# The first cumulative sum of gates: from a TensorE product to a VectorE scan, in the gated stage of a four-layer kernel

## The reference

```python
gk1 = log_sigmoid(x @ Wg1a @ Wg1b + bg1) / 16      # decays of the dense branch, 8 heads x 64
gk2 = log_sigmoid(x @ Wg2a @ Wg2b + bg2) / 16      # of the four routed branches
def chunk_gla(q, k, v, gk, C=64):                  # chunks of 64 tokens
    g = cumsum(gk, axis=1)                         # inside a chunk
    g_last = g[:, -1]
    qg, kg = q * exp(g), k * exp(-g)
    A = tril(qg @ kg.T)
    ...
    return S * exp(g_last) + kv                    # state to the next chunk
o = chunk_gla(q1, k1, v, gk1) + sum_e chunk_gla(q2*w_e, k2*w_e, v, gk2*m_e)
```

## Time and profile before

| | |
|---|---|
| median of three runs | 1802.73 us |
| the profiled execution | 1806.19 us, span 1804.9 us |
| granted TensorE clock, mean over the span | 0.951 |
| TensorE matmul busy | 1556.2 us (86%) |
| VectorE busy | 1275.3 us (71%) |
| ScalarE busy | 1098.3 us (61%) |
| GpSimd busy | 697.8 us (39%) |

### The profile page before, as it was taken

The page is one execution under the profiler, slowest core; times in us unless marked ns, Lnnn a source line. Parts: engine busy times, 40 slices in busy tenths (PEclk is TensorE's granted clock), DMA queues, the critical chain, the costliest instruction groups (busy, mean ns, idle before and its releaser), DMA issues. The chain is left out here.

```text
span 1804.9 us, 45554 instructions
## 1 busy us (share of the span) xinstructions
PE 1556.2 (86%) x19648; PEld 998.5 (55%) x19648; DVE 1275.3 (71%) x2003; ACT 1098.3 (61%) x1641; POOL 697.8 (39%) x499
## 2 busy tenths in 40 slices
PE   3587897899999999999977778888788888899999
PEld 2354566787778778877863232433333343466565
DVE  4656644777777677768767868778777886655665
ACT  3255576777767777786752567677667767533331
POOL 4122300554255344534450556365465545411100
PEclk8789898999999999999997889999999999999999
DMA  7864200000000000000024274246237222223332
GB/s 176 196 165 113 47 5 12 2 2 2 2 2 2 2 1 2 2 1 2 32 88 99 52 212 98 63 133 142 56 107 167 66 64 72 67 71 94 95 96 76
DMA packets 54821, 121.17 MB, mean 67 GB/s; under 512 B 6124, under 2 KB 14468, under 8 KB 53020
## 3 DMA queue, kind: packets, MB, share of 16 engines
q1 hardware_dynamic: 51708, 112.74, 23.7%
q10 hardware_dynamic: 2912, 5.51, 1.8%
HBM read 85.70 MB, written 31.74 MB: 65 GB/s over the span
## 5 line engine op out<-in xcount | busy, mean ns | idle before, releaser
L1445 DVE TENSOR_REDUCE arena<-ring 128x2 f32<-128x1024 f32 (+2 forms) x320 | 342.1, 1110 | 87.9 <-PE ring L1302 62.1
L1545 ACT ACTIVATE arena<-ring 128x1024 f32<-128x1024 f32 (+1 forms) x320 | 291.3, 937 | 135.4 <-PE ring L1331 92.0
L1352 PE MATMUL accs<-arena 128*9 128x512 f32 (+3 forms) x1536 | 174.3, 528 | 3.8 <-ACT arena L1545 3.8
L2509 POOL TENSOR_TENSOR arena<-arena 128x1280 f32<-128x1280 f32 x28 | 65.3, 2332 | 287.0 <-PE accs L2270 231.7
L1295 PE MATMUL ring<-arena 48*128 48x512 bf16 (+3 forms) x768 | 128.8, 347 | 41.8 <-DVE arena L1445 21.1
L1324 PE MATMUL ring<-arena 51*128 51x512 bf16 (+3 forms) x768 | 125.0, 343 | 45.8 <-DVE arena L1445 25.1
L2501 POOL TENSOR_TENSOR arena<-arena 128x512 f32<-128x512 f32 x112 | 141.3, 1294 | 3.0 <-DVE arena L2311 3.0
L287 POOL TENSOR_SCALAR xn<-x,moments,rstd 128x128 f32<-128x128 f32 x80 | 65.0, 825 | 192.3 <-DVE rstd L258 178.3
L2782 ACT ACTIVATE arena<-ring 128x512 f32<-128x512 f32 x80 | 47.7, 596 | 134.8 <-PE ring L2651 132.7
L2494 POOL TENSOR_TENSOR arena<-arena 128x1024 f32<-128x1024 f32 x32 | 86.3, 2698 | 108.1 <-DVE arena L2368 108.1
L1718 POOL TENSOR_TENSOR arena<-arena 128x1024 f32<-128x1024 f32 x28 | 65.9, 2354 | 128.6 <-ACT arena L1558 104.5
(11 more groups left out here) (342 smaller groups left out, 4165.9 us busy)
## 6 DMA issues: line engine op xcount, KB each, us to landing
arena<-whole_k SPq DMA_DIRECT2D x32, 512.0 KB, 4.6
arena<-whole_q SPq DMA_DIRECT2D x32, 512.0 KB, 6.2
arena<-moe_scratch SPq DMA_DIRECT2D x128, 128.0 KB, 2.9
arena<-c_scratch_q SPq DMA_DIRECT2D x14, 384.0 KB, 9.3
arena<-c_scratch_k SPq DMA_DIRECT2D x14, 384.0 KB, 12.2
a_scratch_k<-arena SPq DMA_DIRECT2D x8, 512.0 KB, 4.2
c_scratch_k<-arena SPq DMA_DIRECT2D x8, 512.0 KB, 4.5
arena<-a_scratch_q SPq DMA_DIRECT2D x9, 384.0 KB, 7.2
```

What stands on the lines that cost most here:

```text
L1352: mm = nc.tensor.matmul(acc[ci % 2][32 * h:32 * h + HD + 1, a - c * BANK:BANK], c_values[b % 2][:, j, r * HEADS // 2 + 2 * g + i, :], weig ...
L1445: nc.vector.tensor_reduce(dst, src, AX.X, ALU.max, negate=True).then_inc(c_max_taken.up(item), 1)
L1545: nc.scalar.activation(view(c_probs[wi % 4]), view(ps), ACT.Exp).then_inc(c_weights_made.up(item), 1)
```

## The change

Tile by tile, the first gate is now projected with features on partitions: `z` keeps one matmul of 512 columns for the second gate (L1925) and has four of 128 columns with the operands swapped for the first (L1928). `gk` is unchanged in shape. A new item `run`, VectorE's alone, stands behind `pair` and makes the cumulative sums in place with a scan over tokens: a reduction of each pair's first 64 tokens, its subtraction from the first token (four elements a partition), and a 512-element scan with a mask that restarts it at each pair (L2328, L2331, L2334). `sum, t, 0` has no TensorE part and no ring buffer any more; ScalarE's part reads the scan's result from SBUF, at the same place of the list, and its decays are two instructions. `gk` waits for ScalarE's last read of the tile before. GpSimd sets the mask once.

```diff
@@ z, on TensorE
-                for i in range(2):
-                    rows = slice(64 * (1 - h) + 32 * i, 64 * (1 - h) + 32 * i + 32)
-                    mm = nc.tensor.matmul(ps[:, i * BANK:(i + 1) * BANK], low_of(b, h)[rows, 1, in_half(t)],
-                                          w("b_second", (1 + h) * BANK, (2 + h) * BANK)[rows, :], start=True, stop=True)
+                rows = [slice(64 * (1 - h) + 32 * i, 64 * (1 - h) + 32 * i + 32) for i in range(2)]
+                low = low_of(b, h)[:, 1, in_half(t)]
+                up_gates = w("b_second", (1 + h) * BANK, (2 + h) * BANK)
+                nc.tensor.matmul(ps[:, BANK:2 * BANK], low[rows[1], :], up_gates[rows[1], :], start=True, stop=True)
+                for p in range(PAIRS):
+                    cols = slice(p * P, (p + 1) * P)
+                    mm = nc.tensor.matmul(ps[:, cols], up_gates[rows[0], cols], low[rows[0], :], start=True, stop=True)
...
@@ gk, on VectorE
                     dv.wait_ge(sum_mm, (t - 1, 1))
+                    dv.wait_ge(sum_exp, (t - 1, 0, "decay"))
...
@@ the order
-                round_ = [("pair", i), ("half", n), ("sc", i, 0), ("sc", i, 1), ("k2x", n), ("mx", n), ("mask", i),
+                round_ = [("pair", i), ("run", n), ("half", n), ("sc", i, 0), ("sc", i, 1), ("k2x", n), ("mx", n), ("mask", i),
                           ("sum", n, 0), ("kt", i), ("soft", n), ("fin", i - 1), ("sum", n, 1), ("qk1", n), ("vk", n),
                           ("z", n + 1), ("routed", n), ("kv", i, 0), ("kv", i, 1), ("av", i), ("in", i, 0), ("in", i, 1),
                           ("mid", n), ("gk", n + 1)]
-            on_ring = ("turn", "logits", "rows_hot", "rows_w", "low", "gate", "z", "mx", "vk", "sum", "qk1", "pair", "kt",
+            on_ring = ("turn", "logits", "rows_hot", "rows_w", "low", "gate", "z", "mx", "vk", "qk1", "pair", "kt",
                        "kv", "fin")
...
@@ run, on VectorE
+                    elif kind == "run":
+                        dv.wait_ge(z_step, (t, "gk"))
+                        by_pair = gk[:, 0, :].rearrange("p (a c) -> p a c", a=PAIRS)
+                        nc.vector.tensor_reduce(gk_head[:, :], by_pair[:, :, 0:P // 2], AX.X, ALU.add).then_inc(
+                            z_step.up((t, "head")), 1)
+                        dv.wait_ge(z_step, (t, "head"))
+                        nc.vector.tensor_tensor(by_pair[:, :, 0], by_pair[:, :, 0], gk_head[:, :], ALU.subtract).then_inc(
+                            z_step.up((t, "begin")), 1)
+                        dv.wait_ge(z_step, (t, "begin"))
+                        nc.vector.tensor_tensor_scan(gk[:, 0, :], pair_keep[:, :], gk[:, 0, :], 0.0, ALU.mult, ALU.add).then_inc(
+                            z_step.up((t, "running")), 1)
...
@@ sum 0, on ScalarE
+                    elif kind == "sum" and item[2] == 0:
+                        running = gk[:, 0, :]
+                        ac.wait_ge(z_step, (t, "running"))
+                        if t:
+                            ac.wait_ge(qk_decayed, (t - 1, "k1"))
+                        nc.scalar.activation(up[0][:, :], running, ACT.Exp, scale=1 / NORMALIZER).then_inc(
+                            sum_exp.up((t, 0, "up")), 1)
+                        nc.scalar.activation(dn[0][:, :], running, ACT.Exp, scale=-1 / NORMALIZER).then_inc(
+                            sum_exp.up((t, 0, "down")), 1)
...
+                        nc.scalar.activation(decay[t % 3][:, :, 0, 0], pair_cols(running)[:, :, P - 1], ACT.Exp,
+                                             scale=1 / NORMALIZER).then_inc(sum_exp.up((t, 0, "end")), 1)
+                        nc.scalar.activation(decay[t % 3][:, :, 1, 0], gk_head[:, :], ACT.Exp, scale=1 / NORMALIZER).then_inc(
+                            sum_exp.up((t, 0, "decay")), 1)
```

More of the change, by code:

```diff
@@ L1842, in build @@
         xnT_1 = carve([P, T])
+        pair_keep, gk_head = carve([P, BANK]), carve([P, PAIRS])
         assert used[0] <= SHARED
@@ L1969, in gla_first_dve @@
                     dv.wait_ge(sum_mm, (t - 1, 1))
+                    dv.wait_ge(sum_exp, (t - 1, 0, "decay"))
+                else:
+                    dv.wait_ge(gla_cleared, "pair first")
                 z = ps[:, :].rearrange("p (i c) -> p i c", i=2)
@@ L2067, in beside @@
                 return {k: more.get(k, []) + follow.get(k, []) for k in (*more, *follow)}
-            order = [("z", 0), ("pair", -1), ("gk", 0), ("half", 0), ("k2x", 0), ("mx", 0), ("sum", 0, 0), ("soft", 0), ("sum", 0, 1),
+            order = [("z", 0), ("pair", -1), ("gk", 0), ("run", 0), ("half", 0), ("k2x", 0), ("mx", 0), ("sum", 0, 0), ("soft", 0), ("sum", 0, 1),
                      ("qk1", 0), ("vk", 0), ("z", 1), ("routed", 0), ("gk", 1)]
@@ L2091, in gla @@
             for item in order:
-                if item[0] in on_ring or item[0] == "sc" and item[2] == 0 or (
+                if item[0] in on_ring or item[0] == "sc" and item[2] == 0 or item[0] == "sum" and item[2] == 1 or (
                         item[0] == "next" and item[1] in ("turn", "q", "k")):
@@ L2196, in pe_program @@
                         mm.then_inc(pair_mm.up(t), 1)
[L2197 to L2200, removed]
+                    elif kind == "sum" and item[2] == 1:
                         pe.wait_ge(z_step, (t, "gk"))
-                        if i:
-                            pe.wait_ge(mix_made, (t, "sum"))
-                            pe.wait_ge(mix_half, t)
+                        pe.wait_ge(mix_made, (t, "sum"))
+                        pe.wait_ge(mix_half, t)
                         for p in range(PAIRS):
-                            mm = nc.tensor.matmul(ps[:, p * 256:p * 256 + cols], gk[:, i, p * P:(p + 1) * P], rhs,
+                            mm = nc.tensor.matmul(ps[:, p * 256:p * 256 + P + 2 * ROUTES], gk[:, 1, p * P:(p + 1) * P], mixed[:, :],
                                                   start=True, stop=True)
-                        mm.then_inc(sum_mm.up((t, i)), 1)
+                        mm.then_inc(sum_mm.up((t, 1)), 1)
                     elif kind == "qk1":
@@ new lines, in act_program @@
+                        nc.scalar.activation(decay[t % 3][:, :, 1, 0], gk_head[:, :], ACT.Exp, scale=1 / NORMALIZER).then_inc(
+                            sum_exp.up((t, 0, "decay")), 1)
+                    elif kind == "sum":
+                        v4 = pair_cols(ps[:, :])
+                        ac.wait_ge(sum_mm, (t, 1))
+                        if t:
+                            ac.wait_ge(qk_decayed, (t - 1, "q2"))
+                        nc.scalar.activation(pair_cols(up[1][:, :]), v4[:, :, 0:P], ACT.Exp).then_inc(
+                            sum_exp.up((t, 1, "up")), 1)
+                        nc.scalar.activation(pair_cols(dn[1][:, :]), v4[:, :, 0:P], ACT.Exp, scale=-1.0).then_inc(
+                            sum_exp.up((t, 1, "down")), 1)
+                        if t >= 3 and last_factor(t - 2):
+                            ac.wait_ge(state_step, (last_factor(t - 2), "factor"))
+                        nc.scalar.activation(decay[t % 3][:, :, :, 1:1 + ROUTES],
+                                             v4[:, :, P:P + 2 * ROUTES].rearrange("p a (k d) -> p a k d", k=2),
+                                             ACT.Exp).then_inc(sum_exp.up((t, 1, "decay")), 1)
@@ L2489, in pool_program @@
             def pool_program():
+                nc.gpsimd.memset(pair_keep[:, :], 1.0).then_inc(gla_cleared.up("pair keep"), 1)
+                gp.wait_ge(gla_cleared, "pair keep")
+                nc.gpsimd.memset(pair_cols(pair_keep[:, :])[:, :, 0:1], 0.0).then_inc(gla_cleared.up("pair first"), 1)
                 for item in order:
```

17 lines of the change are left out of this document (2 added, 15 removed).

## The result

The changed kernel takes 1886.74 us (median of six runs, 1885.82 to 1898.08), the kernel before 1803.13 us in the same comparison (six runs): ratio 1.0479, 95% interval 1.0441 to 1.0517. It is slower by 84 us; 61 were forecast (1864 us). The range given eight chances in ten went to 1893; the forecast's own range ended at 1885, and 1886.74 lies just outside it and inside that of rival 3, the clock (1878 to 1910). The forecast had the sign, the place and some three quarters of the size.

What follows compares the result with a forecast made beforehand. VectorE's leg from second queries to first keys, then TensorE's back, bound it; terms of 15.1 us a batch gave 60.5 us on 1806.19, 1866.7, less 3.5 for the median: 1864 us; own range 1845 to 1885, eight in ten 1826 to 1893.

Steps and rivals of the forecast that it cites:

- rival 3: In the gated stage TensorE's clock falls in the new idle stretch: 1878 to 1910 us in all; 20% chance.
- The lock: VectorE instructions with two SBUF operands stand still until GpSimd's current one ends: `run` 2.9 us instead of 1.8.
- The sum, tile by tile: Growth of each tile's round in the gated stage, added up: 15.1 us a batch, 60.5 us for four batches.
- TensorE's new wait for the first mask: Before `fin`, which now reuses the first scores' buffer: start at x + 6.1 instead of x + 4.13, some 3 us idle.
- TensorE just about keeps up with VectorE: After the wait TensorE reaches `kv` at x + 13.3 to 13.5, with VectorE's first keys ending at x + 13.5.
- what it saved comes out as idle time: TensorE's four removed 130-column sums, 1.02 us a round, were to become idle time on TensorE.
- Tile 5's term: Tile 5's round, taken to have some slack: between 0 and 1.9 us longer, put at 1.25.
- the rival's milder form: A third of the rounds lose 1 to 1.7 us from `fin` to `kv` by the slower clock: 11 to 18 us more.
- Two signs that the prediction named as "wrong": Granted clock well under 1.00 in the gated stage; VectorE waiting in front of the first keys. No size given.
- The upper bound of 0.43: Extra time of `z` on TensorE if half of the second band's work is serialised: 0.43 us; 0.1 was taken.
- TensorE as the bound from the start: TensorE bounds the kernel and each round gets 0.6 to 0.9 us shorter: 1774 to 1784 us; 5% chance.
- No lock on the new instructions: `run` on VectorE isn't held up by GpSimd and takes 1.85 us: 28 us more, 1831 us; 14% chance.

Runs made afterwards that it cites:

- the filled kernel: The changed kernel with the eight transposes of `kt` done three times, 1.74 us more TensorE work a round before the first mask: 1869.52 us, ratio 1.0381.

## Why the prediction was right, and where not

- **What bounds the kernel.** Right: VectorE's leg to the first keys, against 94% on TensorE. Moving `run` out of it gave back 71 us, and shortening the leg of the kernel before gained 10 us without removing any work.
- **The lock.** Right, and the walk held to 0.2 us: scan's end 4.91 for 4.95, keys 13.32 for 13.5. That the leg grows by less than the 2.9 us of `run`, because L2408 no longer waits, was right too: 1.8 us (13.32 less 11.55) for the forecast 1.9.
- **The sum, tile by tile.** By how much a round is longer than before, in us; "full clock" is from rounds of the changed kernel without a fall of the clock, or, for tiles 1, 5 and 7, from such rounds of the filled one:

| tile of the batch | forecast | full clock | changed kernel |
|---|---|---|---|
| 0 | 1.9 | 1.8 | 1.8 (0.2 in the first batch) |
| 1 | 3.3 | 3.0 | 2.8 to 4.8 |
| 2 | 1.9 | 1.8 | 1.8 to 3.5 |
| 3 | 1.9 | 1.8 | 1.8 to 3.0 |
| 4 | 1.7 | 2.0 | 2.0 to 4.9 |
| 5 | 1.25 | 2.0 | 3.6 to 5.3 |
| 6 | 1.9 | 1.8 | 1.8 to 2.5 |
| 7 | 1.25 | 1.2 | 2.9 |

  Over the 31 rounds the third column makes some 59 us and the last 87.6. The sum of the forecast, 60.5 for 32 rounds (four times 15.1 is 60.4, and 59.2 for these 31), was the price of the longer leg to 1 us, and the missing 29 us are the clock. With 60.5 the forecast would be 1863 us, not 1864.
- **TensorE's new wait for the first mask.** Right in place and size (2.85 us for some 3). That "TensorE just about keeps up with VectorE" holds at the full clock in tiles 2 and 3, where `kv` follows the keys by 0.1 to 0.2 us; it left out what the slow clock does to TensorE's way from `fin` to `kv`. That "what it saved comes out as idle time" was wrong for most tiles: some 25 of the 30 us above are the saving's, what it spares at the slow clock included.
- **Tile 5's term was too small**: 1.25 us forecast, without a row for the round, and 2.0 at the full clock. In the changed kernel it is 3.6 or 5.3, and the difference is the clock. There the router's product stands between `kt` and `fin` and waits for the mask, and `fin` behind it takes 2.05 us instead of 1.13:

```profile
592.14 2.18 PE L1902 MATMUL ring<-weights_large,xnT 128*128 128x4 f32 x16 [2.85 <-DVE arena L2373]
594.18 2.05 PE L2281 MATMUL ring<-arena,weights_constants 128*128 128x512 f32 x2
```

  That round as a busy-time row, and the same tile of the next batch in the filled kernel, 22.35 us long at a clock of 1.00:

```profile
586.05:610.05 24.00, 20.79 (x260) 17.42 (x258) 17.61 (x36) 13.90 (x28) 10.53 (x7) 0.93 0.01 1
```
```profile
766.87:789.22 22.35, 20.88 (x276) 18.06 (x274) 17.77 (x36) 13.90 (x28) 10.54 (x7) 1.00 0.01 2
```

- **The clock.** It had 20% as a rival beside the forecast, and it is part of the result. 17 us come back when the gap is partly filled, and the rounds put it at 29 in all: more than the rival's milder form (11 to 18 in a third of the rounds), just short of the other (30 to 55 in all of them). Two signs that the prediction named as "wrong" came with it: the granted clock below 1.00 in the stage, and VectorE waiting in front of the first queries and keys (20 times for 41.8 us, where it was 8 for 30.0). As the wait was forecast at the length it has, the clock should have been a term of the sum. That the time still fell in the range of eight in ten is owed to the width given for this rival, not to the sum.
- **`z`.** Taken at 0.1 us more, measured 0.03 (1.09 us for 1.06). The upper bound of 0.43 can't be worked out from the row given for it, where 1.13 less 0.64 is 0.49.
- **Rivals 1 and 2.** TensorE as the bound from the start: no, the kernel got slower; the saving pays in the time only with the leg shortened. No lock on the new instructions: no, the scan takes 2.25 us in the median and 1.22 where GpSimd waits for it.

What stays open: why the clock falls in some rounds and not in others with the same idle stretch. The division into 59 and 29 us compares rounds of one execution of each kernel; the filling by itself gave back 22 us of the stage, since it leaves 1.12 us of the gap and three rounds with a slow stretch, the first and two of tile 5's.

## What to carry to other kernels

Work moved to a less busy engine costs what its place there costs, not its share of busy time: find the stretch of that engine on which the others wait, and put the work in the other one, at a point where its inputs are there. When an instruction is inserted in front of the release of a shared buffer, follow who takes that buffer next and what stands behind it there. And where VectorE and GpSimd share a stretch, move VectorE's products of two SBUF tensors out of it before anything else.

## What the runs showed of the hardware

A four-element subtraction of two SBUF operands (0.17 us free, up to 0.93) and a 512-element scan on VectorE waited for GpSimd's current instruction like large products do, and GpSimd's next one went between them. The scan took 1224 ns free and 2249 in the median beside GpSimd, in the same program. In the changed kernel the granted clock fell to 0.50 behind 12 of the 20 idle stretches of 2.85 us in TensorE, behind all four of 3.31 in tile 1's rounds and behind all three of 1.86 in tile 7's. Four matmuls of 128 columns in one 32-row band ran beside one of 512 columns in the other at no cost (1.09 us for 1.06). And 1.74 us of useless transposes made a kernel 17 us faster whose TensorE otherwise idled for 2.85 us in most rounds.
